# Convolution, attention and pixel attention of eight images: a rebuilt passage from one image to the next

## The reference

```
ll, lh, hl, hh = half the sums and differences of the four pixels of each 2x2 square   # 128 x 1024 each
attention on ll:  q, k, v = qkv_w @ ll (8 heads of 16); q, k normalised per pixel;
                  scores 1024 x 1024 per head; the 512 largest of each row kept; softmax; times v
                  proj_w, group norm
high bands:       depthwise 3x3 convolution of the 3 x 128 channels lh, hl, hh;
                  group norm, silu, pointwise 384 x 384, group norm; h + alpha * y
inverse transform (a, b, c, d from ll, lh, hl, hh), add to x (scaled);
ffn:              w1 (128 to 256), group norm, gelu, w2, group norm, add
```

## Time and profile before

| | us |
|---|---|
| median of three executions | 6547.7 |
| the profiled execution: device time | 6551.84 |
| its span, first to last instruction | 6550.0 |
| PE busy in the span | 5096.8 (78%) |
| DVE busy | 4551.3 (69%) |
| ACT busy | 4574.2 (70%) |
| POOL busy | 412.2 (6%) |
| mean granted TensorE clock | 0.886 |

### The profile page before, as it was taken

The page is one execution under the profiler, slowest core; times in us unless marked ns, Lnnn a source line. Parts: engine busy times, 40 slices in busy tenths (PEclk is TensorE's granted clock), DMA queues, the critical chain, the costliest instruction groups (busy, mean ns, idle before and its releaser), DMA issues.

```text
span 6550.0 us, 92687 instructions
## 1 busy us (share of the span) xinstructions
PE 5096.8 (78%) x30756; PEld 3132.4 (48%) x30756; DVE 4551.3 (69%) x8207; ACT 4574.2 (70%) x6939; POOL 412.2 (6%) x135
## 2 busy tenths in 40 slices
PE   5343878876888868878788868887688778885788
PEld 2000445653666435553455435664356535563466
DVE  1676479954898469973898559974789649894443
ACT  3885389945998379954999369973799559993223
POOL 3000300011000200012000200003000110000000
PEclk8555889987999879998899879998799879997899
DMA  1001100011000110011000110001100120002000
GB/s 49 6 9 40 51 16 15 14 50 55 13 15 13 56 47 18 16 52 55 9 18 13 48 55 15 18 33 55 28 16 15 50 54 13 16 13 61 9 7 12
DMA packets 109767, 187.72 MB, mean 29 GB/s; under 512 B 48768, under 2 KB 53760, under 8 KB 106144
## 3 DMA queue, kind: packets, MB, share of 16 engines
q1 hardware_dynamic: 109216, 181.05, 9.1%
HBM read 110.61 MB, written 69.47 MB: 27 GB/s over the span
## 4 chain that ended last, share of the span: by engine, by line
DVE 33%; PE 25%; issue 19%; ACT 12%; DMA 5%; SPq 3%; POOL 2%; DVEq 1%; ACTq 0%; POOLq 0%
DVE MX L1400 9%; ACT work L891 7%; PE PS L493 6%; DVE arena L1378 6%; DVE M L1300 5%; PE PS L741 5%; PE PS L462 4%; DVE work L1292 3%; DVE work L1260 3%; DVE work L1284 2%; ACT work L909 2%; PE PS L434 2%; PE PS L405 2%; PE PS L645 2%; PE PS L480 1%
## 5 line engine op out<-in xcount | busy, mean ns | idle before, releaser
L891 ACT ACTIVATE work<-arena,T 128x1024 bf16<-128x1024 f32 x1792 | 2039.7, 1140 | 96.7 <-DVE T L1247 63.9
L493 PEld LDWEIGHTS PS<-V,work 128*128 128x128 f32 x16384 | 2011.1, 194 | 119.8 <-ACT work L916 29.1
L493 PE MATMUL PS<-V,work 128*128 128x129 f32 x16384 | 2040.1, 278 | 22.4 <-ACT work L916 22.4
L1400 DVE TENSOR_REDUCE MX<-PS 128x1 f32<-128x512 f32 x2048 | 1406.4, 687 | 682.8 <-PE PS L462 673.5
L916 ACT ACTIVATE work<-PS 128x1024 f32<-128x1024 f32 x1024 | 1039.6, 1015 | 407.0 <-PE PS L480 406.2
L462 PE MATMUL PS<-KP,QP 96*128 96x512 bf16 x2048 | 854.1, 417 | 511.2 <-DVE MX L1400 388.0
L1378 DVE SCALAR_TENSOR_TENSOR arena<-PS,work 128x1024 f32<-128x1024 f32 x512 | 624.2, 1219 | 260.2 <-ACT work L909 260.2
L462 PEld LDWEIGHTS PS<-KP,QP 96*128 96x128 bf16 x2048 | 201.8, 99 | 1094.3 <-DVE MX L1400 922.4
L881 ACT ACTIVATE arena<-PS 128x1024 f32<-128x1024 f32 x512 | 520.8, 1017 | 264.0 <-PE PS L405 262.9
L480 PE MATMUL PS<-QP,KP 99*128 99x512 bf16 x2048 | 621.1, 385 | 62.6 <-ACT work L916 36.7
L1300 DVE MAX8 M<-work 128x8 f32<-128x1024 f32 x512 | 625.1, 1221 | 3.2
(11 more groups left out here) (176 smaller groups left out, 3858.3 us busy)
## 6 DMA issues: line engine op xcount, KB each, us to landing
work<-scr SPq DMA_DIRECT2D x768, 32.0 KB, 1.8
work<-in_x SPq DMA_DIRECT2D x8, 2048.0 KB, 8.1
arena<-in_x SPq DMA_DIRECT2D x8, 2048.0 KB, 7.9
scrX<-arena SPq DMA_DIRECT2D x8, 2048.0 KB, 6.4
XR<-scrX SPq DMA_DIRECT2D x64, 256.0 KB, 2.7
out<-YO SPq DMA_DIRECT2D x64, 256.0 KB, 2.0
scr<-work SPq DMA_DIRECT2D x24, 512.0 KB, 3.8
scrL<-work SPq DMA_DIRECT2D x24, 512.0 KB, 9.5
```

Of the source, the lines that this page charges most:

```text
L493: last = mm(PS[:, 5 + i // 2, 136 * (i % 2):136 * (i % 2) + 129], P1[:, (16 * j + k) % 3, t, 128 * i:128 * i + 128], V1[:, mt, :], start=( ...
L891: A(JKA[:, m % 2, :], scores(h, i), ACT.Sign, scale=-1.0, bias=T[:, h % 2, i:i + 1], accum_out=CA[:, h % 2, i:i + 1]).then_inc(s["ca"], 1)
L1400: V.reduce_max(MX[:, c % 2, i, w:w + 1], PS[:, 4, :], AX.X).then_inc(s["mr"], 1)
```

## The change

- **Convolution.** `NPE = 1`: only band 0 is convolved on PE. Bands 1 and 2 are made on DVE from the padded bands by nine instructions each (`taps`): the first multiplies a shifted window by its weight, the other eight multiply and add in place. Their statistics are read from SBUF, and their copies from PSUM on ACT are gone.
- **Recombination.** `mix` and `base` (ten DVE instructions) move out of the boundary into pass 7 and pass 8 of the slots, and x and the bands are fetched at the start of SP's pass 7. The corners are now in XQ, `add0` writes into X1, which moved.
- **Heads stored stacked.** The planes of q and k go to DRAM in the order in which the six terms are stacked, by 12 stores (one for each use) in place of three; a head comes back with 2 DMAs instead of 12. Layer 1's planes come back with 7 DMAs instead of 12. The sums OD of a head are stored with one DMA ahead of the head's four, instead of four behind them. OC and OB of the first seven heads are fetched in pass 8, those of head 7 in the boundary.
- **Next x in halves**: the upper half after head 7's threshold rows in pass 7, the lower after its last mask in pass 8. The band LL on POOL now waits for the product OC x OB, since OB lies over it.
- **Head 0 ahead of the maxima.** PE computes all eight score tiles of head 0 before the first `maxima` of chunk 0, and no longer waits for the pointwise part (`hs`, `de`) there; that wait stands at the first product with V1.
- **Orders.** The lists of the boundary are written anew on every engine; PSUM banks are dealt out differently. On POOL the power instruction of the group norm of FFN 1 stands ahead of the 128 x 128 power instruction, not behind it.

The diff at its core:

```diff
+NPE = 1
...
-        X1 = units(0, 4)
-        DL, GX, GA, GS = arena[:, 4:7, :], arena[:, 7:11, :], units(11, 1), units(14, 1)
-        OC, OB, DL0 = units(12, 1), units(13, 1), units(14, 1)
+        XQ, DL, GA = units(0, 4), arena[:, 4:7, :], units(7, 1)
+        DL0, X1 = units(4, 1), units(12, 4)
+        OC, OB = places(11, 1), places(9, 1)
         HF = units(4, 8).rearrange("p (o n) -> p o n", o=2)
-        F2 = units(12, 4)
+        F2 = HF[:, 1, :]
         Q1 = units(8, 1)
...
-            def load_x(b):
-                sp.dma_start(Xin, x[bass.ds(b, 1)].rearrange("a c n -> c (a n)")).then_inc(s["xin"], 16)
+            def load_x(b, part):
+                sp.dma_start(Xin[:, 2 * N0 * part:2 * N0 * part + 2 * N0],
+                             x[bass.ds(b, 1), :, 2 * N0 * part:2 * N0 * part + 2 * N0].rearrange("a c n -> c (a n)")).then_inc(s["xin"], 16)
 
             def load_parts(b):
                 sp.wait_ge(s["pv"], b * (NH * NT) + (NH - 1) * NT)
-                sp.dma_start(X1, x[bass.ds(b, 1)].rearrange("a c n -> c (a n)")).then_inc(s["xl"], 16)
+                sp.dma_start(XQ, x[bass.ds(b, 1)].rearrange("a c n -> c (a n)")).then_inc(s["xl"], 16)
...
             def load_head(h):
-                for j, (tq, tk) in enumerate(TERMS):
-                    for w, t in enumerate((tq, tk)):
-                        sp.dma_start(QK0[16 * j:16 * j + 16, h % 3, w, :], scr0[t, w, 16 * h:16 * h + 16, :]).then_inc(s["hq%d" % (h % 3)], 16)
+                done = s["hq%d" % (h % 3)]
+                for w in range(2):
+                    sp.dma_start(QK0[0:KS, h % 3, w, :], scr0[w, h].rearrange("j d n -> (j d) n")).then_inc(done, 16)
+
+            def store_planes(n, t, made):
+                sp.wait_ge(s[made], (n + 1) * 2)
+                for j, pair in enumerate(TERMS):
+                    for w in range(2):
+                        if pair[w] == t:
+                            sp.dma_start(scr0[w, :, j, :, :], PT[:, t, w * N0:w * N0 + N0]).then_inc(s["scrw"], 16)
+
+            def load_done(b, first):
+                if first:
+                    sp.wait_ge(s["od"], (b * NH + NH - 1) * 80)
+                    rows, heads = slice(0, 112), slice(0, NH - 1)
+                else:
+                    sp.wait_ge(s["od"], (b + 1) * (NH * 80))
+                    rows, heads = slice(112, 128), slice(NH - 1, NH)
+                sp.dma_start(OC[rows], scrO[heads].rearrange("h d n -> (h d) n")).then_inc(s["ol"], 16)
+                if first:
+                    sp.wait_ge(s["odr"], (b * NH + NH - 1) * 16)
+                else:
+                    sp.wait_ge(s["odr"], (b + 1) * (NH * 16))
+                sp.dma_start(OB[rows],
...
             def store_head(b, h):
                 sp.wait_ge(s["o"], b * NH + h + 1)
+                sp.dma_start(OD[:, h % 2, :], OT[HD:128:32, h % 2, :].rearrange("q (j e) -> q j e", e=8)).then_inc(s["od"], 16)
                 for q in range(4):
-                    sp.dma_start(scrO[h:h + 1, :, 256 * q:256 * q + 256].rearrange("h d n -> (h d) n"),
-                                 OT[32 * q:32 * q + HD, h % 2, :]).then_inc(s["od"], 16)
-                for q in range(4):
-                    sp.dma_start(OD[32 * q:32 * q + 32, h % 2, :],
-                                 OT[32 * q + HD:32 * q + HD + 1, h % 2, :].rearrange("p (j e) -> p j e", e=8))\
-                        .then_inc(s["od"], 16)
...
+                    if l0 and h == NH - 1:
+                        load_parts(b)
+                    if l0 and h == NH:
+                        load_done(b, True)
+                        if more:
+                            sp.wait_ge(s["p"], (b + 1) * (NH * NT))
+                            sp.sem_inc(s["free"], 1)
+                            load_x(b + 1, 0)
...
+                    if l0 and h == NH - 1 and more:
+                        load_x(b + 1, 1)
...
+                    q, k = scr1[:, 0:16, :], scr1[:, 16:32, :]
+                    for dst, src in ((QP1[0:32], q[0].unsqueeze(0).to_broadcast([2, 16, N1])), (KP1[0:32], k[0:2]),
+                                     (QP1[32:64], q[1].unsqueeze(0).to_broadcast([2, 16, N1])), (KP1[32:64], k[0:2]),
+                                     (QP1[64:96], q[0:3:2]), (KP1[64:80], k[2]), (KP1[80:96], k[0])):
+                        sp.dma_start(dst, src).then_inc(s["qp1"], 16)
...
+                def first():
+                    for i in range(2, NT):
+                        score(0, i)
+                    for k in range(32):
+                        maxima(0, k)
...
+                    if k == 0 and j == 0 and l0:
+                        pe.wait_ge(s["hs"], (b + 1) * 2)
+                        pe.wait_ge(s["de"], (b + 1) * 6)
...
+                def mix(h, t):
+                    if not l0 or h != NH - 1:
+                        return
+                    D = [DL[:, o, :] for o in range(3)]
+                    if t == "a":
+                        dve.wait_ge(s["dld"], (b + 1) * 48)
+                        cp.did(V.tensor_tensor(GA, D[2], D[0], ALU.subtract))
+                    elif t == "s":
+                        cp.wait(made["a"])
+                        cp.did(V.tensor_tensor(D[0], D[0], D[2], ALU.add))
+                    elif t == 0:
+                        cp.wait(made["s"])
+                        cp.did(V.tensor_tensor(D[2], GA, D[1], ALU.subtract))
+                    elif t == 2:
+                        cp.wait(made[0])
+                        cp.did(V.scalar_tensor_tensor(GA, GA, -1.0, D[1], ALU.mult, ALU.subtract))
+                    elif t == 1:
+                        cp.wait(made["b0"])
+                        cp.did(V.tensor_tensor(D[2], D[1], D[0], ALU.subtract))
+                    else:
+                        cp.wait(made[1])
+                        cp.did(V.tensor_tensor(D[0], D[0], D[1], ALU.add))
+                    made[t] = cp.n
+
+                def base(h, k):
+                    if not l0 or h != NH - 1:
+                        return
+                    dve.wait_ge(s["xl"], (b + 1) * 16)
+                    cp.wait(made[k])
+                    v = corner(k)
+                    g = GA if k == 2 else DL[:, 0 if k == 3 else 2, :]
+                    cp.did(V.scalar_tensor_tensor(v, v, 1.2, g.rearrange("p (y x) -> p y x", x=HH), ALU.mult, ALU.add))
+                    made["b%d" % k] = cp.n
+
+                def based(h):
+                    if not l0 or h != NH - 1:
+                        return
+                    cp.wait()
...
+                def first():
+                    centre(0, 0)
+                    centre(0, 1)
+                    for k in range(24):
+                        maxima(0, k)
+                        if k in (5, 8, 13, 17):
+                            g = (5, 8, 13, 17).index(k)
+                            update(0, g // 2, g % 2)
...
+                def taps(k, t):
+                    if not opn:
+                        return
+                    v = PAD[:, k, t // 3:t // 3 + HH, t % 3:t % 3 + HH]
+                    w = w_dw[:, 9 * k + t:9 * k + t + 1]
+                    o = Y[:, k, :].rearrange("p (y x) -> p y x", x=HH)
+                    if t == 0:
+                        dve.wait_ge(s["pad"], (n + 1) * 3)
+                        ch.did(V.tensor_scalar(o, v, w, None, ALU.mult))
+                    else:
+                        ch.wait(tap[k])
+                        ch.did(V.scalar_tensor_tensor(o, v, w, o, ALU.mult, ALU.add))
+                    tap[k] = ch.n
+                    if t == 8:
+                        ch.wait()
+                        dve.sem_inc(s["dc%d" % k], 1)
...
                     eight(h, 5)
+                    mix(h, "a")
                     apart(h, 7)
...
                         pool.wait_ge(s["pimg"], 4)
+                        if fin:
+                            pool.wait_ge(s["oc"], f + 1)
                         TT(LL, DW[:, 0, :], DW[:, 1, :], ALU.add).then_inc(s["ll"], 1)
...
                 bands(3)
+                power(f, n, fin, opn, 3)
                 norms()
+                power(f, n, fin, opn, 1)
                 repeat()
-                power(f, n, fin, opn, 3)
-                power(f, n, fin, opn, 1)
                 power(f, n, fin, opn, 4)
                 power(f, n, fin, opn, 2)
```

More of the change, by code:

```diff
@@ L587, in slots @@
                     l1_weigh(h - 1, 14)
+                for h in range(-1, NH + 1):
+                    if h == 0:
+                        first()
+                    elif h >= 1:
+                        search(h)
                     maxrow(h)
@@ L1503, in slots @@
                     threshold(h)
+                    mix(h, 2)
+                    base(h, 2)
                     maxima(h + 1, 14)
@@ L1520, in slots @@
                     mask(h, 2)
+                    mix(h, 3)
                     maxima(h + 1, 23)
+                for h in range(-1, NH + 1):
+                    if h == -1:
+                        first()
```

(7 more changed lines are left out.)

415 lines of the change are left out of this document (190 added, 225 removed).

## The result

The changed kernel takes 6527.6 us in the median of nine runs (6520.4 to 6533.4), the kernel before 6549.7 (6547.7 to 6552.1, nine runs on the same chip): ratio 0.9965, 95% interval 0.9955 to 0.9975. It is faster by 22 us. The prediction said 6379, between 6222 and 6450. The direction was right, the size was not: of 169 us forecast, 30.5 came in the profiled executions (span 6550.0 and 6519.5).

What follows compares the result with a forecast made beforehand. The boundary is bound by one engine at a time, a chain to be walked. Seven boundaries at 20.7 us, opening 12 and last boundary 12 make 169 off 6551.8: 6383, shown median 6379; range 6222 to 6450 for eight in ten.

Steps and rivals of the forecast that it cites:

- Planes' fetch: Silu to maxima: store to fetch 3.4 us, fetch 10 to 13, planes ready at silu + 50, hidden behind score tiles.
- RN holds DVE from 1462.8 to 1483.6: FFN 1's norm to gelu: the 128 x 128 power on POOL stalls two-input DVE instructions 20.8 us; bounds 0 and 20.8.
- Product done 12.4 behind the copy-out: Boundary's start: sums stored first, reciprocal after 4.4 us, heads' product done at 1418 instead of 1423.4; gain 5.4 us.
- Product to FFN 1, 22.5 us: Boundary: 9.5 us from product to normed projection, then 13.1 us of PE work until FFN 1 starts at 1440.5.
- FFN 1 to gelu and gelu to silu, without a hold: 22.8 and 20.2: Middle of the boundary if RN holds nothing: gelu starts at 1463.3, silu at 1483.5.
- Mixes ahead of the threshold: Pass 7: three mixes and one base ahead of head 7's threshold make the boundary's start 4.6 us later.
- The row, 46.2: Chunk 0's row of maxima: 46.2 us instead of 48.4, as three gaps of 0.74 for score tiles are gone.
- Opening, 12, bounds 0 and 31: Before the first search pass: points and key ones done at 121 instead of 133.3; gain 12 us, 31 without a lock.
- Scores ahead: Before the first maxima: head 0's eight score tiles take 17.4 us on PE, ending at silu + 55.6; they hide the transfer.
- the walk without a hold: Boundary times if RN holds nothing: row done 179.7 us behind head 7's copy-out; 6227 us in all; chance 20 in 100.
- RN does not hold DVE: Rival: in the boundary taps run beside the power, 19 us more gained each time; 6227 us in all; chance 20 in 100.
- another wait that I count as hidden: Rival, shared with dear taps: points or planes take 13 us more per boundary; 6486 us in all; chance 13 in 100.

Runs made afterwards that it cites:

- e1: The changed kernel with layer 1's planes stored and fetched as before the change (three contiguous stores, twelve fetches in 2 KB pieces): 6353.7 us.
- e3: The kernel before the change, with layer 1's planes stored and fetched in the new form: 6735.4 us, ratio 1.0275.
- f1: The changed kernel with its new scratch layout and stores, but the seven planes' fetches replaced by twelve of 16 rows of 8 KB: 6408.8 us.
- g1: On e1, SP issues heads 1 and 2 and the 2 MB of scrX behind layer 1's planes instead of ahead: 6327.9 us.
- r1: On e1, VectorE waits before the last operand of FFN 1's norm until the 128 x 128 power RN is done: 6465.2 us.
- s1: On g1 with six score tiles among the maxima (6314.0 us): finished heads fetched a pass earlier, head 7's rows and sums stored before x's half: 6290.4 us.
- m1: On g1 with six score tiles among the maxima (6314.0 us): no mix or base of pass 7 ahead of head 7's threshold: 6282.7 us.
- g3: On g1 with six score tiles among the maxima (6314.0 us): layer 1's planes in seven stores and eight fetches of 96 partitions: 6279.2 us.

## Why the prediction was wrong

It was wrong above all in two terms of opposite sign, and right in what it was built on: the boundary is one chain, and what is taken off that chain comes off the time. By its own steps:

- *Planes' fetch ("SP is free: 3.4 + 10 to 13").* This step failed, and it decides. The 3.4 and 14.7 were rows of the old form of the transfer, carried over to a new form because that has fewer DMAs and larger pieces. The diff changed the outermost dimension of the stores from 128 to 4 and of most fetches from 16 to 2. Measured: 17.4 + 29.6. The planes were there at silu + 82.5, not + 50, and silu to maxima took 82.5 us instead of 55.6, 26.9 too little a boundary. e1, e3 and f1 show it from three sides. "SP is free" failed by itself too: in e1, with the old form, store to fetch is still 10.2 us (3.8 in g1, where heads 1 and 2 and scrX go out later), and silu to maxima 63.1, 7.5 of the 26.9. The last boundary, forecast 12 us shorter, became 20.1 longer, of which these are 22.9.
- *"RN holds DVE from 1462.8 to 1483.6."* False: `SH` took 0.16 us inside RN, the sign that the prediction had named for it. The 1.80 us of the earlier trace rows belonged to a band, an operation of 1.89 us on 1024 elements a partition, and was carried to a power, 21.66 us on 128. The price was nearly right (r1: 15.4 us a period for a forced wait); had only this step failed, the time would have come out at the low end, 6227. It hid the first error: 26.9 too little and 19.0 too much make 7.9. The Trainium skill's rule (page "SBUF — State Buffer", section "Who interferes with whom") fits the bands here and not the power.
- *Product done 12.4 behind the copy-out.* Measured 17.7. The walk put the sums at 4.4 us, and they took 11.9: 0.9 MB of heads and sums and 1 MB of x had been issued ahead of them (s1: 4.1 without). The walk counted x only at scrD. That s1 comes so near to 4.4 is luck as far as the reason goes: the walk had it from OD being stored first, and the semaphore waits for all five stores.
- *Product to FFN 1, 22.5 us.* Measured 25.1: 14.9 to the normed projection instead of 9.5, with three holds by bands (1.63, 2.27, 2.67 us) instead of one, and 10.2 from there to FFN 1 instead of 13, since band 0 starts on PE 3.2 us ahead of the projection.
- *FFN 1 to gelu and gelu to silu, without a hold: 22.8 and 20.2.* Measured 24.4 and 20.8. FFN 1's records take 0.44 (26 in 11.32 us), the upper level. But behind its statistics six records of band 0 take 4.28 us, 0.71 each, at a granted clock of 0.65 (1430.84 to 1435.04), and the broadcast of FFN 1's norm stands behind them on PE. Its power was done at 1433.2, so it comes 1.8 us late. At 0.43 a record the six would be through at 1433.4, an estimate: the lower clock makes up the 1.6 us. A tap takes 1.28 us, 1.16 predicted, but the taps are not what silu waits for: the convolution's variance is ready at 1453.3 and its power starts behind RN, at 1454.85.
- *Mixes ahead of the threshold, 4.6.* 3.9 by m1. *The row, 46.2:* 46.2. *Opening, 12, bounds 0 and 31:* 19.4 to head 0's first score tile.
- *Scores ahead.* The eight tiles took 16.9 us (17.4 predicted), but PE first stood 6.4 us, not in the walk. With the planes late that cost nothing.

The six records and the broadcast, in the timeline of PE after:

```profile
1430.84 4.28 PE L778 MATMUL PS<-PAD,diag 128*128 128x512 f32 x6
1435.05 0.81 PE L671 MATMUL PS<-GG,indT 32*128 32x2 f32 x4
```

Against the walk without a hold the boundary is longer by 5.3 + 2.6 + 1.6 + 0.6 + 26.9 = 37.0 us, which is 216.7 - 179.7. Two of the rivals were thus true at once, "RN does not hold DVE" and "another wait that I count as hidden", and the prediction had given them 20 and 13 in 100 as alternatives; for the second it went to 13 us a boundary, half of what it was.

## What to carry over

A transfer whose shape is changed is a new transfer: take its time from no row of the old one, and read its outermost dimension on both sides before its bytes. Take a hold from a row of the same two instructions: here a row for a band said nothing of a power on the same engine. Look what a semaphore counts before an order of stores is given a worth. Where several hidden waits are assumed, price the case that two of them fail together, and order the queue so that what the chain waits for is issued ahead of the bulk.

## What the runs showed of the hardware

- Five of the seven fetches of layer 1's planes, with an outermost dimension of 2, ran at 51 GB/s on 2 of 16 engines (after), and the stores, with a 4, at 91 GB/s on 4. With 16 rows a fetch it was 115 to 123 GB/s, in pieces of 8 KB (f1) or 2 KB (e1), and with 96 rows 261 (g3).
- Beside a power on GpSimd of 21.66 us a two-input operation of VectorE took 0.16 us and its taps 1.28; beside bands on GpSimd operations on one element a partition lasted 1.6 to 2.7 us (after).
- PE stood 6.4 us ahead of head 0's first score tile where the loop jumps back, and not at all in the two steady boundaries without a jump (after); 3.2 when 2 MB of stores and two heads' fetches were issued later (g1). The view names no releaser.
- Behind 32 short records (squares, 3.6 us at clock 1.00) and 0.25 us of idleness PE's granted clock fell from 1.00 to 0.50, the lower level, near 1432; six records took 0.71 us each instead of 0.43 (after).
